# Transposing quantised rows with the rounding constant still in them, and a router read in pairs

## The reference

```python
x = x + tanh(g_xattn[0]) * state_space(ctx, layernorm(x))     # "M"
x = x + tanh(g_ffn[0])   * quantised_ffn(layernorm(x))        # "F0"
x = x + tanh(g_xattn[1]) * attention_16_heads(layernorm(x), ctx)   # "A1"
x = x + tanh(g_ffn[1])   * experts_16_top_4(layernorm(x))     # "F", layer 1
x = x + tanh(g_xattn[2]) * map_attention(ctx, layernorm(x))
x = x + tanh(g_ffn[2])   * gated_ffn_hadamard(layernorm(x))   # "F", layer 2
x = x + tanh(g_xattn[3]) * map_attention(ctx, layernorm(x))
x = x + tanh(g_ffn[3])   * experts_8_top_2(layernorm(x))      # "F", layer 3

def quantised_ffn(x):          # weights rounded to -1, 0, 1; H = 256, I = 1024
    gate = silu(qlinear(x, w_gate)); up = qlinear(x, w_up)
    return qlinear(gate * up, w_down)
def qlinear(x, w):
    s = max|x| over a row / 127 + 1e-5
    xq = clip(round(x / s), -128, 127)
    return (xq @ wq.T) * s * ws
```

## Time and profile before

| | us |
|---|---|
| median of 3 runs | 1005.11 |
| lowest, highest | 1002.9, 1006.55 |
| the profiled execution | 1004.66 |
| its span | 1002.9 |

### The profile page before, as it was taken

How to read it: one execution, slowest core, us unless ns; L and a number is a source line. 1 busy time by engine, 2 the same in 40 slices (tenths; PEclk the granted TensorE clock), 3 DMA queues, 4 the chain that set the end, 5 groups by cost and what they waited for, 6 DMA issues and landing times.

```text
span 1002.9 us, 15717 instructions
## 1 busy us (share of the span) xinstructions
PE 912.1 (91%) x5336; PEld 747.2 (75%) x5336; DVE 715.4 (71%) x1303; ACT 642.6 (64%) x1246; POOL 492.7 (49%) x488
## 2 busy tenths in 40 slices
PE   6477677668999999999989999999999999999998
PEld 2133233346999999999968888888888888888887
DVE  6899998986777777777667675796666655666544
ACT  5767765766777777777655666756667544554553
POOL 1487561126766666666443443454344544444442
PEclk8599989798999999999999999999999999999999
DMA  9200100003000000000019511211112500021221
GB/s 346 115 1 0 63 1 0 1 1 159 1 2 2 1 1 1 1 2 1 1 51 339 181 53 46 61 64 54 46 58 56 232 1 1 1 74 53 62 65 45
DMA packets 17612, 56.26 MB, mean 56 GB/s; under 512 B 3073, under 2 KB 4201, under 8 KB 15389
## 3 DMA queue, kind: packets, MB, share of 16 engines
q1 hardware_dynamic: 5341, 34.27, 9.0%
q10 hardware_dynamic: 12192, 20.98, 7.1%
HBM read 54.08 MB, written 1.16 MB: 55 GB/s over the span
## 4 chain that ended last, share of the span: by engine, by line
PE 50%; DVE 13%; POOL 8%; issue 7%; ACT 3%; ACTq 1%; DMA 1%; DVEq 0%; POOLq 0%
PE psum L434 14%; PE psum L436 14%; PE psum L435 14%; POOL a_P L2020 3%; DVE a_max L1718 2%; POOL a_rk L1941 2%; POOL a_rq L1949 2%; DVE psum L1654 1%; PE psum L843 1%; DVE psum L1854 1%; PE psum L769 1%; PE psum L700 1%; DVE bn_st L1315 1%; PE psum L803 1%; ACT L1133 1%
## 5 line engine op out<-in xcount | busy, mean ns | idle before, releaser
L434 PE MATMUL psum<-x_norm_T_hi,f_wgu_hi 128*128 128x512 f32 x400 | 160.3, 401 | 3.2 <-DVE f_h_lo L1861 3.2
L436 PE MATMUL psum<-x_norm_T_hi,f_wgu_lo 128*128 128x512 f32 x400 | 157.5, 394 | 0.0
L435 PE MATMUL psum<-x_norm_T_lo,f_wgu_hi 128*128 128x512 f32 x400 | 156.8, 392 | 0.0
L434 PE MATMUL psum<-f_wd_hi,f_h_hi 128*128 128x256 f32 x400 | 121.9, 305 | 0.1
L1654 DVE TENSOR_TENSOR psum<-f_silu,psum 128x512 f32<-128x512 f32 x100 | 69.3, 693 | 69.5 <-PE psum L436 47.2
L436 PE MATMUL psum<-f_wd_hi,f_h_lo 128*128 128x256 f32 x400 | 112.9, 282 | 0.0
L435 PE MATMUL psum<-f_wd_lo,f_h_hi 128*128 128x256 f32 x400 | 112.9, 282 | 0.0
L1861 DVE TENSOR_TENSOR f_h_lo<-psum,f_h_hi 128x512 fp32r<-128x512 f32 x100 | 68.9, 689 | 51.6 <-ACT f_h_hi L889 51.1
L1954 POOL TENSOR_TENSOR f_wgu_lo<-f_w,f_wgu_hi 128x512 fp32r<-128x512 f32 x44 | 56.7, 1290 | 94.3 <-ACT f_wgu_hi L889 94.3
L1954 POOL TENSOR_TENSOR f_wgu_lo<-f_wb,f_wgu_hi 128x512 fp32r<-128x512 f32 x36 | 46.6, 1293 | 103.5 <-ACT f_wgu_hi L889 103.5
L2057 POOL TENSOR_TENSOR m_dBu<-m_du,m_Bs 128x1024 f32<-128x1024 f32 x31 | 73.0, 2355 | 35.1 <-DVE m_inv L1480 16.1
(11 more groups left out here) (328 smaller groups left out, 2635.1 us busy)
## 6 DMA issues: line engine op xcount, KB each, us to landing
f_cw<-r_rows ACTq DMA_DIRECT2D x38, 256.0 KB, 3.3
f_wb<-in_f1b SPq DMA_DIRECT2D x6, 1152.0 KB, 9.7
f_w<-in_f3w SPq DMA_DIRECT2D x1, 5376.0 KB, 16.6
f_wa<-in_f1a SPq DMA_DIRECT2D x1, 3840.0 KB, 11.8
w_raw<-in_w0raw SPq DMA_DIRECT2D x1, 3072.0 KB, 14.9
f_w<-in_f2w SPq DMA_DIRECT2D x2, 1536.0 KB, 8.6
f_cw<-r_rows ACTq DMA_DIRECT2D x12, 224.0 KB, 3.0
f_cw<-r_rows ACTq DMA_DIRECT2D x12, 192.0 KB, 2.9
```

Source lines behind the costliest of these rows:

```text
L434: mm(out, wh, xh, start=start, stop=False, **kw)
L435: mm(out, wh, xl, start=False, stop=False, **kw)
L436: return mm(out, wl, xh, start=False, stop=stop, **kw)
```

## The change

The quantised rows of the hidden layer are transposed as `h0a`, four-byte values with the rounding constant still added, into two banks (4 and 5); ScalarE's copy subtracts the constant through its bias. `within_8_bits` and `hq` go. The waits on `q_hq` become waits on `q_r` or `q_hTp`. The upper parts of the key weights move from ScalarE to VectorE, behind the scales of the passes 4 to 7. Key unit 0 moves from bank 4 to bank 6, from pass 7 to pass 8, behind the wait for the last product; the transposes for A1 use the banks 4 and 5; the first queries lie in bank 4 (`query_bank`). `quantised_inputs(0)` is issued ahead of the wait of g = 31 in M, and ScalarE applies Silu to one scratch value right behind its copy. The router's upper and lower weights become one tile, read as one moving operand of 64 columns.

```diff
-    wrh, wrl = (place("fixed", f"r_w_{n}", [P, KC, 32], f32r) for n in ("hi", "lo"))
+    wrs = place("fixed", "r_w_parts", [P, KC, 2, 32], f32r)
+    wrh, wrl = wrs[:, :, 0, :], wrs[:, :, 1, :]
...
-    KEY_BANKS = (4, 2, 3, 7)
+    KEY_BANKS = (6, 2, 3, 7)
+    def query_bank(i):
+        return 6 if i else 4
...
                 if g + 3 < 2 * NS:
                     broadcast_B(g + 3)
+                if g == NS + 15:
+                    loaded(pe, "identb")
+                    pe.wait_ge(S("wvo_copied"), HEADS - 1)
+                    quantised_inputs(0)
                 if g:
                     pe.wait_ge(S("m_hC"), g)
...
-                if g == NS + 15:
-                    loaded(pe, "identb")
-                    pe.wait_ge(S("wvo_copied"), HEADS - 1)
-                    quantised_inputs(0)
...
-                pe.wait_ge(S("q_hq"), t + 1)
+                pe.wait_ge(S("q_r"), t + 1)
                 if t == NT - 1:
                     pe.wait_ge(S("a_kT"), 1)
+                    pe.wait_ge(S("a_rqs"), 1)
+                if t == 1:
+                    pe.wait_ge(S("q_xT"), 2)
...
-                    last = nc.tensor.transpose(psb[:, 5, j * P:(j + 1) * P], hq[:, j * P:(j + 1) * P], identb[:, :])
+                    last = nc.tensor.transpose(ps[:, 4 + j // 4, j % 4 * P:(j % 4 + 1) * P], h0a[t % 2][:, j * P:(j + 1) * P], ident[:, :])
...
                 if t == 3:
-                    pe.wait_ge(S("m_res"), 2)
+                    pe.wait_ge(S("q_hT"), 1)
                     quantised_inputs(1)
...
-                if t == NT - 1:
+                if t == NT:
                     pe.wait_ge(S("a_ctx"), 1)
                     pe.wait_ge(S("a_wk"), 1)
-                    key_unit(0, KEY_BANKS[0])
-                if t == NT:
                     pe.wait_ge(S("q_sg"), 2 * NT)
...
                 if t == NT:
                     pe.wait_ge(S("q_h"), 2 * NT)
+                    key_unit(0, KEY_BANKS[0])
                     key_unit(3, KEY_BANKS[3]).then_inc(S("a_k"), 1)
...
-                    transpose_norm(0, ("A1", 0), (6, 5))
+                    transpose_norm(0, ("A1", 0), (4, 5))
...
-                    last = mm3(ps[:, 7, t * 32:(t + 1) * 32], xh[:, c, sl], xl[:, c, sl], wrh[:, c, :], wrl[:, c, :],
-                               c == 0, c == KC - 1)
+                    mm(ps[:, 7, t * 64:(t + 1) * 64], xh[:, c, sl], wrs[:, c, :, :].rearrange("p a n -> p (a n)"), start=c == 0, stop=False,
+                       skip_group_check=True)
+                    last = mm(ps[:, 7, t * 64:t * 64 + 32], xl[:, c, sl], wrs[:, c, 0, :], start=False, stop=c == KC - 1, skip_group_check=True)
...
             quantised_inputs(0)
+            A(scratch[:, 22:23], epsc[:, :], ACT.Silu)
...
-                copy(hqT[:, :, :].rearrange("p j t -> p (j t)"), psb[:, 5, :]).then_inc(S("q_hT"), 1)
+                A(hqT[:, :, :].rearrange("p j t -> p (j t)"), ps[:, 4:6, :].rearrange("p a b -> p (a b)"), ACT.Identity,
+                  bias=nmagic[:, :]).then_inc(S("q_hT"), 1)
...
-                if SPLIT_AT <= t < SPLIT_AT + 4:
-                    sl = slice((t - SPLIT_AT) * HALF, (t - SPLIT_AT + 1) * HALF)
-                    copy(wkh[:, sl], wk[:, sl]).then_inc(S("a_wkh"), 1)
...
-            def within_8_bits(t):
-
-                dve.wait_ge(S("q_r"), t + 1)
-                if t:
-                    dve.wait_ge(S("q_hTp"), t)
-                V.tensor_scalar(hq[:, :], h0a[t % 2][:, :], MAGIC, 127.0, ALU.subtract, ALU.min).then_inc(S("q_hq"), 1)
...
-                if 0 < t < NT - 1:
-                    within_8_bits(t - 1)
+                if SPLIT_AT <= t < NT:
+                    sl = slice((t - SPLIT_AT) * HALF, (t - SPLIT_AT + 1) * HALF)
+                    if t == SPLIT_AT:
+                        loaded(dve, "wq", "wk")
+                    V.tensor_copy(wkh[:, sl], wk[:, sl]).then_inc(S("a_wkh"), 1)
...
-            V.tensor_copy(rl[:, :, 0:nl], ps[:, 7, 0:TH * 32].rearrange("p (t n) -> p t n", t=TH)[:, :, 0:nl]).then_inc(S("b7_free"), 1)
+            parts_ = ps[:, 7, 0:TH * 64].rearrange("p (t n) -> p t n", t=TH)
+            link(V.tensor_copy(rl[:, :, 0:nl], parts_[:, :, 32:32 + nl]))
+            V.tensor_tensor(rl[:, :, 0:nl], parts_[:, :, 0:nl], rl[:, :, 0:nl], ALU.add).then_inc(S("b7_free"), 1)
```

More of the change, by code:

```diff
@@ L145, in flamingo_kernel @@
     h0a = [place("Bf", f"q_ha{i}", [P, I0]) for i in range(2)]
-    hq = place("Bf", "q_hq", [P, I0], bf16)
+    at["Bf"] += 2048
     hqT = place("Bf", "q_hqT", [P, I0 // P, P], bf16)
@@ L671, in keys_queries @@
                     pe.wait_ge(S("a_rqs"), i)
+                if i == 1:
+                    pe.wait_ge(S("a_ktok"), 3)
                 for c in range(KC):
-                    last = mm3(ps[:, 6, :], hi[:, c * P:(c + 1) * P], lo[:, c * P:(c + 1) * P], xh[:, c, :], xl[:, c, :],
+                    last = mm3(ps[:, query_bank(i), :], hi[:, c * P:(c + 1) * P], lo[:, c * P:(c + 1) * P], xh[:, c, :], xl[:, c, :],
                                c == 0, c == KC - 1)
@@ L677, in keys_queries @@
                     pe.wait_ge(S("a_kT"), i)
-                    if i == 1:
-                        pe.wait_ge(S("a_ktok"), 3)
                     pe.wait_ge(S("a_wk"), min((i + TH - 1) // TH, 3) + 1)
@@ L699, in query_sums @@
                 for t in range(TH):
-                    last = mm(ps[:, 6, t:t + 1], qsq[:, t * P:(t + 1) * P], ones[:, 0:1], start=True, stop=True)
+                    last = mm(ps[:, query_bank(i), t:t + 1], qsq[:, t * P:(t + 1) * P], ones[:, 0:1], start=True, stop=True)
                 last.then_inc(S("a_qn"), 1)
@@ L1053, in rounded_hidden @@
                 if i >= 2:
-                    act.wait_ge(S("q_hq"), i - 1)
+                    act.wait_ge(S("q_hTp"), i - 1)
                 A(h0a[i % 2][:, :], h0[i % 2][:, :], ACT.Identity, scale=qt[i % 2][:, 2:3], bias=magic[:, :]).then_inc(S("q_r"), 1)
@@ L1164, in squares @@
                     act.wait_ge(S("a_qn"), i)
-                A(qsq[:, :], ps[:, 6, :], ACT.Square).then_inc(S("a_qsq"), 1)
+                A(qsq[:, :], ps[:, query_bank(i), :], ACT.Square).then_inc(S("a_qsq"), 1)
                 if i > 1:
                     act.wait_ge(S("a_s"), i - 1)
-                copy(qh[i % 2][:, :], ps[:, 6, :]).then_inc(S("a_qh"), 1)
+                copy(qh[i % 2][:, :], ps[:, query_bank(i), :]).then_inc(S("a_qh"), 1)
             def keys_hi(i):
@@ L1181, in attn1 @@
             last_hidden_round, last_hidden_copy = last_hidden
-            norm_T(1, (6, 5), xTh)
+            norm_T(1, (4, 5), xTh)
             squares(0)
@@ L1186, in attn1 @@
             loaded(act, "ctk")
-            act.wait_ge(S("q_hq"), NT - 1)
+            act.wait_ge(S("q_hTp"), NT - 1)
             copy(ctkh[:, :, :], ctk[:, :, :]).then_inc(S("a_ctkh"), 1)
@@ L1549, in ffn0 @@
                     stats(0)
-                    within_8_bits(NT - 2)
                 for n in range(2):
@@ L1562, in ffn0 @@
                     first_key_norms()
-                    x_lo(1, (6, 5), xTh, xTl)
+                    x_lo(1, (4, 5), xTh, xTl)
                     first_head_scaled()
@@ L1584, in ffn0 @@
             output(NT - 3)
-            return (lambda: within_8_bits(NT - 1)), (lambda: output(NT - 2)), (lambda: output(NT - 1))
+            return (lambda: output(NT - 2)), (lambda: output(NT - 1))
         def first_key_norms():
@@ L1665, in queries_lo @@
                 dve.wait_ge(S("a_qh"), i + 1)
-                V.tensor_tensor(ql[i % 2][:, :], ps[:, 6, :], qh[i % 2][:, :].bitcast(f32), ALU.subtract).then_inc(S("a_ql"), 1)
+                V.tensor_tensor(ql[i % 2][:, :], ps[:, query_bank(i), :], qh[i % 2][:, :].bitcast(f32), ALU.subtract).then_inc(S("a_ql"), 1)
             def keys_scaled(i):
@@ L1678, in query_norms @@
                     dve.wait_ge(S("a_rq"), i)
-                V.tensor_copy(rqs[:, :], ps[:, 6, 0:TH]).then_inc(S("a_rqs"), 1)
+                V.tensor_copy(rqs[:, :], ps[:, query_bank(i), 0:TH]).then_inc(S("a_rqs"), 1)
             def keys_lo(i):
@@ L1698, in attn1 @@
             other_heads_scaled(0, 3)
-            for step in last_outputs[:2]:
-                step()
+            last_outputs[0]()
             for i in range(HEADS2):
@@ L1736, in attn1 @@
                 if i == 0:
-                    last_outputs[2]()
+                    last_outputs[1]()
                     dve.wait_ge(S("q_out"), NT)
```

## The result

| | before | after |
|---|---|---|
| median, us | 1004.94 | 999.1 |
| lowest to highest, us | 1002.9 to 1006.55 | 997.77 to 1000.65 |
| ratio, 95% interval | | 0.9943 [0.9931, 0.9955] |
| profiled execution, us | 1004.66 | 999.48 |
| its span, us | 1002.9 | 997.7 |

The changed kernel is 5.7 us faster (4.5 to 6.9); 999.3 was forecast. I read its profile in the order of the prediction. First the busy times of the stretches that answer to those of before: us, busy of PE, PEld, DVE, ACT, POOL, then granted clock, DMA, GB/s.

A forecast was written before the change was run, and what follows sets the result against it. VectorE was taken to bound the quantised stage, ScalarE close behind, and saturated TensorE most of the rest. 1.7 + 0.5 + 1.75 - 1.8 + 3.4 = 5.55 us off 1004.66 gave 999.1, median 999.3, range 995.8 to 1002.9 us.

The forecast's parts named there:

- Start of the stage: Quantised stage's beginning: earlier transposes and Silu table load bring the first product forward, 1.7 us gained (1.28 to 1.75).
- Tiles 0 to 3: First quantised tiles: the removed subtraction mostly turns into waiting, against longer four-byte transposes; 0.5 us gained, between 0 and 1.8.
- Tiles 4 to 7: Later quantised tiles: VectorE loses a subtraction and gains a weight copy; 1.75 us gained, 1.0 with the dear copy.
- The tail: Last product to first heads: moved key unit, last weight copy and four-byte transposes lose 1.8 us (1.2 to 2.7).
- Router pairs: Half routings: four of twelve matmuls go in eight places on saturated TensorE; 3.4 us gained (2.6 to 3.6).
- Rival 1: Quantised stage gives nothing, another engine taking VectorE's place or tail costs at upper bounds; 1001.5 us, chance 0.15.
- Rivals 2 and 3: Weight copies and GpSimd meet in all four tiles, 1001.6 us, chance 0.07; router pairs gain nothing, 1002.7, chance 0.06.
- Rival 4: First heads, 228 to 246 us: lower TensorE clock costs up to 9.8 us, 1009 us; chance 0.05.
- rival 5: More gain than forecast: tiles 0 to 3 give 1.8 us, tail costs 1.2; 997.4 us or less, chance 0.12.

The follow-up runs named there:

- x_start: The kernel before with only the early Silu table load and the moved transposes of the first quantised rows; 1004.41 us, ratio 0.9991 [0.9981, 1.0002].
- x_router: The kernel before with only the router's matmul pairs changed; 1000.49 us, ratio 0.9959 [0.9948, 0.9971].
- x_stage: The changed kernel without the router pairs, early table load and moved transposes; 1005.36 us, ratio 1.0002 [0.9994, 1.0011].
- x_no_router: The changed kernel with the router's twelve matmuls of a half put back; 1004.38 us, ratio 0.999 [0.998, 0.9999].

## Why the prediction was right

The table and the single parts let each term be judged. The signs that were named came: the table load ahead of 167 us, steps of 4.24, 3.99 and 6.10 us, eight matmuls in 0.80 us, and, counted from the last state-space product, the first queries' lower part 2.9 us earlier (some 3 forecast).

**Start of the stage, 1.7 us.** It measured 1.79 in every trace that has both edits, and by the mechanism described: silu no longer waits for the table, and the first product starts the moment `gated(1)` ends (169.85 + 1.29 = 171.14). The table load showed no drain, as the row said. By the page ScalarE: Activation LUTs of the Trainium skill, section What ACT_TABLE_LOAD costs, up to 1.4 us more would have come; no trace here shows any of it. That these 1.79 us reach the end of the program isn't shown: x_start gained 0.9 us (-0.2 to 1.9).

**Tiles 0 to 3, 0.5 us.** The number came out in the pair of profiles (22.36 us to 21.84 between the products of tile 0 and tile 4), but its cause didn't. x_router has the old code in this stretch and took 21.66 us, at a mean granted clock of 0.84; before took 22.36 at 0.69; x_stage has the new code and took 21.68 at 0.84. At the same clock the edit gives nothing. Step by step, product to product, x_router took 6.70, 5.81, 4.81 and 4.34 us and x_stage 6.70, 5.70, 4.91 and 4.37; before differs from x_router in the fourth alone, 5.04, where its clock was at the lower level up to 192.4 us. VectorE's busy time in the stretch fell from 20.64 us in before to 18.95 in after and turned into waiting altogether. This is the step that failed: the term of 0.5 us measured 0.

**Tiles 4 to 7, 1.75 us.** It measured 16.06 - 14.33 = 1.73, with steps of 4.24, 3.99 and 6.10 for 4.2, 4.0 and 6.1. The copy was priced at 0.43 us, 0.36 in the step; it took 0.43 and 0.34. No copy met GpSimd in this execution. The rule of locking out (SBUF — State Buffer, section Who interferes with whom, in the Trainium skill) was not put to the test by the change; the one old meeting went on showing 1.26 us in x_router, with the subtraction at 197.26 and GpSimd's instruction at 196.71.

**The tail, -1.8 us.** The first queries' lower part lost 14.11 - 12.92 = 1.19 us (0.7 + 0.36 = 1.06 predicted), the second head's queries 20.31 - 18.26 = 2.05 (1.8). The key unit's share is seen whatever the clock: the transposes of the normalised rows begin 5.49 to 5.51 us behind the last product in the four traces with the old code and 6.27 us in after, x_stage and x_no_router, 0.78 us later for 0.7 predicted. At the first maximum of attention the loss is 1.57 in this pair; over all traces with the old code in the tail, d is 24.44 to 24.91, with the new code 25.23 to 26.51 (after, x_stage, x_no_router), on average 1.2 more. So the term may have been somewhat dear, within its bounds.

**Router pairs, 3.4 us.** If anything too small. The pairs gave 4.1 us alone and 4.7 in the changed kernel, each with more than 1 us of interval; in the traces 4.2 (x_router) and 3.6 (x_no_router to after: from 2.40 us late at 470 us to 1.20 early at the end). A half went from 489.24–490.49, 1.25 us, to 0.80 us: 0.45 x 8 = 3.6. The forecast lies in both intervals of the medians. I had taken 0.1 off for halves that end in another wait; by the traces there was nothing to take off.

**Sum.** By the stretches: 1.79 + 2.25 - 1.57 = 2.47 in the stage, 0.73 lost before it by the executions' own difference, and 3.5 for the rest, mostly the routings: 5.2 us of span. Counted from the last state-space product, after is 2.11 us ahead of before at the first routing. The stage's 2.47 is more than the 1.0 us (0.1 to 2.0) that x_no_router gained by its median, and so is the 1.7 + 0.5 + 1.75 - 1.8 = 2.15 of the forecast. Without the clock's share in tiles 0 to 3 the edits are worth 1.8 + 0 + 1.7 - 1.6 = 1.9. What part of the remaining 0.9 is noise of the medians and what is given back behind the stage stays open. So the total, 5.55 us forecast and 5.7 measured, is nearer than its parts: by the medians the stage with its start gave 1.0 for 2.15 and the router pairs 4.7 for 3.4. The mechanisms held but for the tiles 0 to 3; that these two differences cancel to 0.2 us is luck.

**The rivals.** Rival 1, that the stage gives nothing, fits x_stage's median, where the early start was missing; against it for stage and start together stands x_no_router, barely (0.1 to 2.0 us). Rivals 2 and 3 are out by the rows above. Rival 4's condition wasn't met: the mean clock of the stretch from 226 to 244.3 us was 0.78 for 0.85, well above the 0.61 from which the gain would have been cancelled. Of rival 5, the 1.8 us in the tiles 0 to 3 didn't come; the tail at 1.2 is about the mean of the traces.

## What to carry to other kernels

Where TensorE is saturated and its matmuls are narrow, count the instructions, not their columns: with 32 or 64 moving columns one matmul less was worth 0.11 us each of 32 times, and this was about two thirds or more of the whole gain. With 512 columns the pitch was 0.23 us (209.57 to 209.81 above), so there the columns count. A gain in a stage where the clock moves should be measured from an event inside the program and between executions with the same clock there, otherwise a term gets the credit for the clock. Three engines were within some per cent of the same busy time here, and moving the weight copies from one to the other moved a trace by a microsecond and the median by nothing that could be told.

## What the runs showed of the hardware

**The clock's dips fall on different instructions from execution to execution.** After and x_no_router run the same instructions up to the first routing. Yet the last state-space product came at 166.47 us in the one and 165.17 in the other; over all the traces it came between 165.17 and 167.73. Here are four matmuls on TensorE and the table of 5 us around them, first in after, then in x_no_router:

```profile
107.62 3.56 PE L476 MATMUL psum<-m_u,m_diag_D 128*128 128x512 f32 x4 [0.81 <-DVE m_u L1473]
```

```profile
105.00:110.00 5.00, 2.98 (x5) 1.07 (x5) 5.00 (x7) 2.93 (x4) 2.38 (x2) 0.79 0.03 11
```

```profile
107.01 1.98 PE L475 MATMUL psum<-m_u,m_diag_D 128*128 128x512 f32 x4 [0.81 <-DVE m_u L1471]
```

```profile
105.00:110.00 5.00, 3.38 (x8) 1.53 (x9) 5.00 (x6) 2.56 (x4) 2.80 (x2) 1.00 0.00 0
```

The same four take 3.56 or 1.98 us, with the granted clock of the stretch at 0.79 or 1.00. Everything behind waits for them: after was 0.61 us behind x_no_router ahead of them, and VectorE's next scan starts 2.31 us later, of which 1.0 comes back at 146 us. This is as large as most parts of this change.

**The four-byte transposes.** Eight of 128x128 values lasted 1.04 us at the full clock and 1.91 at the lower level; eight two-byte ones lasted 0.62 (in before at 212.88 us) and 1.08. At the full clock this is 0.4 us more per tile, which I had worked out and which TensorE's idle time held.
